# Two score products on the two halves of TensorE's rows, with 49 contracted rows each in place of 65

## The reference, cut to what matters

```python
# layer 0 (dist is (1, 512, 512), one scale per head)
scores = jnp.einsum('bhqd,bhkd->bhqk', q, k) / np.sqrt(hd)
scores = scores - torus_dist[:, None, :, :] * torus_scale[None, :, None, None]
scores = jnp.where(pad, NEG_INF, scores)
attn = jax.nn.softmax(scores, axis=-1)
# layer 1 (its mask lets in only keys of the last 128, for these inputs)
scores = jnp.einsum('bhnd,bhmd->bhnm', q, k) * scale
scores = jnp.where(mask, scores, -jnp.inf)
attn = jax.nn.softmax(scores, axis=-1)
```

## Time and profile before

| | before |
|---|---|
| median of 3 runs | 1530.71 us |
| the profiled execution | 1530.74 us |
| span of its trace | 1528.9 us |
| PE busy | 1372.1 us (90%) |
| DVE, ACT, POOL busy | 866.8, 803.0, 692.0 us |
| granted TensorE clock, mean | 0.96 |
| score matmuls L657 (layer 0) | 512, busy 205.3 us |
| score matmuls L703 (layer 1) | 512, busy 100.1 us |

### The profile page before, as it was taken

One profiled execution on the slowest core, in us unless ns is written; L12 is line 12 of the kernel. 1 busy time (PEld: TensorE's weight loads), 2 busy tenths in 40 slices (PEclk: granted clock), 3 DMA queues, 4 the chain that ended last, 5 costly groups with the idle time before them and its releaser, 6 DMA issues.

```text
span 1528.9 us, 25914 instructions
## 1 busy us (share of the span) xinstructions
PE 1372.1 (90%) x9365; PEld 1090.1 (71%) x9365; DVE 866.8 (57%) x2296; ACT 803.0 (53%) x1266; POOL 692.0 (45%) x856
## 2 busy tenths in 40 slices
PE   5898999999999999999999978898979888888867
PEld 3666777777777777777777767676767677767655
DVE  3766647548548457466556454647384746465551
ACT  3556655756746746656657526362535444453611
POOL 2788767758658758668768510101010101010110
PEclk9999999999999999999999989998999998999988
DMA  8654426325425534345263275856665747474510
GB/s 252 109 112 76 92 29 98 84 30 98 98 41 79 103 55 72 84 76 98 37 117 85 29 161 84 180 89 137 93 154 73 160 62 166 56 158 79 69 42 14
DMA packets 102537, 142.56 MB, mean 93 GB/s; under 512 B 22114, under 2 KB 49906, under 8 KB 102402
## 3 DMA queue, kind: packets, MB, share of 16 engines
q1 hardware_dynamic: 102402, 140.82, 49.6%
HBM read 98.27 MB, written 41.98 MB: 92 GB/s over the span
## 4 chain that ended last, share of the span: by engine, by line
PE 56%; DVE 18%; ACT 12%; POOL 7%; issue 3%; DMA 2%; SPq 1%; DVEq 0%; ACTq 0%; POOLq 0%
PE dense L589 15%; PE dense L569 13%; PE turned L669 9%; DVE shifted L1082 5%; PE pv L684 5%; PE score L657 4%; POOL shifted L472 3%; PE score L703 3%; ACT hidden L853 2%; PE turned L712 2%; POOL bias L465 2%; ACT L853 2%; DVE stats L968 2%; ACT L888 2%; DVE x_norm L978 2%
## 5 line engine op out<-in xcount | busy, mean ns | idle before, releaser
L1082 DVE CUSTOM_DVE_ANT_0 shifted<-score,bias 128x512 f32<-128x512 f32 x512 | 332.7, 687 | 258.4 <-PE score L657 156.8
L472 POOL TENSOR_SCALAR shifted<-shifted,row_max 128x512 f32<-128x512 f32 x512 | 358.3, 712 | 222.1 <-DVE row_max L1082 219.9
L872 ACT ACTIVATE probs<-turned 128x512 f32<-128x512 f32 x512 | 278.1, 596 | 213.3 <-PE turned L669 211.7
L669 PE MATMUL turned<-ident,shifted 128*128 128x128 f32 x2048 | 269.7, 274 | 7.5 <-POOL shifted L472 6.8
L669 PEld LDWEIGHTS turned<-ident,shifted 128*128 128x128 f32 x2048 | 233.3, 141 | 56.5 <-issue 26.7
L589 PE MATMUL dense<-w_down,hidden 128*128 128x256 f32 x1024 | 247.0, 385 | 12.1 <-ACT hidden L853 12.1
L465 POOL TENSOR_SCALAR bias<-dist,scale 128x1024 f32<-128x1024 f32 x192 | 218.4, 1138 | 21.0 <-DMA down_bias<-in_L_cond_b 21.0
L657 PE MATMUL score<-k_rows,q_rows 65*128 65x512 f32 x512 | 205.3, 456 | 23.6 <-DVE row_max L1082 10.5
L589 PEld LDWEIGHTS dense<-w_down,hidden 128*128 128x128 f32 x1024 | 185.6, 191 | 51.1 <-issue 16.3
L569 PE MATMUL dense<-feat_m,w_up 128*128 128x512 f32 x768 | 192.7, 404 | 8.4 <-DVE feat_m L1046 6.1
L888 ACT ACTIVATE probs<-turned 128x512 f32<-128x512 f32 x128 | 76.4, 597 | 202.8 <-PE turned L712 202.4
(11 more groups left out here) (114 smaller groups left out, 1556.6 us busy)
## 6 DMA issues: line engine op xcount, KB each, us to landing
q_rows<-qk_halves SPq DMA_DIRECT2D x256, 128.0 KB
k_rows<-qk_halves SPq DMA_DIRECT2D x256, 128.0 KB
qk_halves<-qk_high SPq DMA_DIRECT2D x64, 256.0 KB, 3.0
qk_halves<-qk_low SPq DMA_DIRECT2D x64, 256.0 KB, 3.0
x_in_t<-in_x SPq DMA_DIRECT2D x8, 512.0 KB, 3.6
x_res<-in_x SPq DMA_DIRECT2D x8, 512.0 KB, 8.3
x_mid<-x_norm SPq DMA_DIRECT2D x8, 512.0 KB, 3.5
x_in_t<-x_mid SPq DMA_DIRECT2D x8, 512.0 KB, 9.1
```

The costliest lines, as they stand in the source:

```text
L472: ins = pool.tensor_scalar(shifted[:, u % 3, i, :], shifted[:, u % 3, i, :], -1.0, row_max[:, t % 6:t % 6 + 1], ALU.mult, ALU.add)
L669: mm = pe.transpose(turned_bank[z % 2][:, HALF * kk + P * i:HALF * kk + P * i + P], shifted[:, u % 3, i, P * kt:P * kt + P], ident[:, :])
L872: act.activation(probs[:, u % RING, 2 * pair:2 * pair + 2, :], turned_bank[z % 2][:, :].rearrange("p (a c) -> p a c", a=2), ACT.Exp)\
L1082: dve.tensor_tensor_reduce(shifted[:, u % 3, i, :], score_bank[t % 2], bias[:, u % 2, i, :], 1.0, 3.0e38, ALU.add, ALU.min, row_max[:, t % ...
```

## The change

The product low·low is dropped: `TERMS` lists three combinations, so a score contracts 3 × 16 + 1 = 49 rows. These fit into one half of the partitions, and the operands now lie there twice: keys and mask on partitions 0 to 48 and again on 64 to 112 (a strip is 64 partitions); of the queries, even tiles lie on the first strip and odd tiles on the second. A unit's two matmuls take one strip each and write one bank each; so do the heads' four matmuls, in the order first, second, first, second. TensorE waits once per unit, until VectorE has read both tiles of the unit before. A group is now loaded with 12 DMAs for q (128 columns each), 6 for k and 2 for the mask. The ones of the mask row are set by two memsets of 32 partitions in place of one of a single partition, and the mask is built on partition 0.

```diff
-    KROWS = 4 * HD
+    TERMS = ((0, 0), (0, 1), (1, 0))
+    KROWS = len(TERMS) * HD
+    STRIP = P // 2
-    ROWS_LOADED = 9 * 16
+    ROWS_LOADED = 2 * (3 * len(TERMS) + 1) * 16
...
-        q_rows = sb("q_rows", [KROWS + 1, 2, HG, L], F32R)
-        k_rows = sb("k_rows", [KROWS + 1, 2, HG, L], F32R)
+        q_rows = sb("q_rows", [P, 2, HG, HALF], F32R)
+        k_rows = sb("k_rows", [P, 2, HG, L], F32R)
...
-                for r in range(4):
-                    sp.dma_start(q_rows[HD * r:HD * r + HD, g % 2, :, :].bitcast(F32),
-                                 qk_halves[m, r // 2, 0, rows, :].rearrange("(h e) n -> e h n", e=HD))\
+                for e in range(2):
+                    for r, (x, y) in enumerate(TERMS):
+                        at = slice(STRIP * e + HD * r, STRIP * e + HD * r + HD)
+                        for a in range(2):
+                            sp.dma_start(q_rows[at, g % 2, :, P * a:P * a + P].bitcast(F32),
+                                         qk_halves[m, x, 0, rows, P * (2 * a + e):P * (2 * a + e) + P]
+                                         .rearrange("(h e) n -> e h n", e=HD)).then_inc(loaded, 16)
+                        sp.dma_start(k_rows[at, g % 2, :, :].bitcast(F32),
+                                     qk_halves[m, y, 1, rows, :].rearrange("(h e) n -> e h n", e=HD))\
+                            .then_inc(loaded, 16)
+                    at = STRIP * e + KROWS
+                    sp.dma_start(k_rows[at:at + 1, g % 2, :, :].bitcast(F32),
+                                 mask_neg[:, :].bitcast(F32).unsqueeze(1).broadcast_to([1, HG, L]))\
                         .then_inc(loaded, 16)
...
             def scores(n, u):
                 g, half, j = u // 8, u // 4 % 2, u % 4
+                if n > 0 or u > 0:
+                    pe.wait_ge(s["scores_used"], TILES * n + 2 * u)
                 for i in range(2):
-                    t = 2 * u + i
-                    if n > 0 or t > 1:
-                        pe.wait_ge(s["scores_used"], TILES * n + t - 1)
-                    q0 = HALF * half + P * i
-                    pe.matmul(score_bank[t % 2], q_rows[:, g % 2, j, q0:q0 + P],
-                              k_rows[:, g % 2, j, :], start=True, stop=True).then_inc(s["scores_ready"], 1)
+                    at = slice(STRIP * i, STRIP * i + KROWS + 1)
+                    pe.matmul(score_bank[i], q_rows[at, g % 2, j, P * half:P * half + P],
+                              k_rows[at, g % 2, j, :], start=True, stop=True).then_inc(s["scores_ready"], 1)
...
                 for t in range(TT):
-                    mm = pe.matmul(score[:, t // 2, HALF * (t % 2):HALF * (t % 2) + HALF],
-                                   q_rows[:, g % 2, j, P * t:P * t + P], k_rows[:, g % 2, j, L - HALF:L],
-                                   start=True, stop=True)
+                    at = slice(STRIP * (t % 2), STRIP * (t % 2) + KROWS + 1)
+                    mm = pe.matmul(score[:, t % 2, HALF * (t // 2):HALF * (t // 2) + HALF],
+                                   q_rows[at, g % 2, j, P * (t // 2):P * (t // 2) + P],
+                                   k_rows[at, g % 2, j, L - HALF:L], start=True, stop=True)
```

More of the change, by code:

```diff
@@ L127, in build @@
         score_bank = [score[:, i, :] for i in range(2)]
-        head_scores = score[:, :, :].rearrange("p a b -> p (a b)").rearrange("p (t k) -> p t k", t=TT)[:, :, HALF - P:HALF]
+        head_scores = score[:, :, :].rearrange("p b (a k) -> p a b k", a=2)[:, :, :, HALF - P:HALF]
         turned_bank = [ps(f"turned{i}") for i in range(2)]
@@ L179, in build @@
         rstd = sb("rstd", [P, 2, TT])
-        mask_row = sb("mask_row", [KROWS + 1, L], U8)
-        mask_neg = sb("mask_neg", [KROWS + 1, L], F32R)
+        mask_row = sb("mask_row", [1, L], U8)
+        mask_neg = sb("mask_neg", [1, L], F32R)
         mask_col = sb("mask_col", [P, TT], U8)
@@ L294, in load_mask @@
                 rows = d["mask_BxS_bf1"] if m < B else d["mask_BxS_bk0"]
-                sp.dma_start(mask_row[KROWS:KROWS + 1, :], rows[m % B:m % B + 1, :]).then_inc(s["mask_loaded"], 16)
+                sp.dma_start(mask_row[:, :], rows[m % B:m % B + 1, :]).then_inc(s["mask_loaded"], 16)
                 if m >= B:
@@ L317, in load_group @@
                 rows = slice(HG * HD * g, HG * HD * (g + 1))
-                for r in range(4):
-                    sp.dma_start(q_rows[HD * r:HD * r + HD, g % 2, :, :].bitcast(F32),
-                                 qk_halves[m, r // 2, 0, rows, :].rearrange("(h e) n -> e h n", e=HD))\
-                        .then_inc(loaded, 16)
[L322 to L327, removed]
+                for e in range(2):
[11 more added lines that the diff above has]
+                                 mask_neg[:, :].bitcast(F32).unsqueeze(1).broadcast_to([1, HG, L]))\
+                        .then_inc(loaded, 16)
             def next_mask(m):
@@ L375, in prologue @@
                 load_x(1)
-                sp.wait_ge(s["ones_set"], 1)
+                sp.wait_ge(s["ones_set"], 2)
                 store_half(0, 0)
@@ L478, in mask @@
                 pad = -PAD if m < B else PAD
-                pool.tensor_scalar(mask_neg[KROWS:KROWS + 1, :], mask_row[KROWS:KROWS + 1, :], pad, -pad,
+                pool.tensor_scalar(mask_neg[:, :], mask_row[:, :], pad, -pad,
                                    ALU.mult, ALU.add).then_inc(s["mask_ready"], 1)
@@ L512, in prologue @@
                 pool.wait_ge(s["pool_consts"], 3)
-                pool.memset(q_rows[KROWS:KROWS + 1, :, :, :].bitcast(F32), 1.0).then_inc(s["ones_set"], 1)
-                pool.wait_ge(s["ones_set"], 1)
+                for e in range(2):
+                    pool.memset(q_rows[STRIP * e + 32:STRIP * e + STRIP, :, :, :].bitcast(F32), 1.0)\
+                        .then_inc(s["ones_set"], 1)
+                pool.wait_ge(s["ones_set"], 2)
                 mask(0)
@@ L761, in prologue @@
                 pe.wait_ge(s["value_ones"], 1)
-                pe.wait_ge(s["ones_set"], 1)
+                pe.wait_ge(s["ones_set"], 2)
             def turn(n):
@@ L1114, in shift_head @@
                 dve.wait_ge(s["scores_ready"], TILES * n + TT * h + TT)
-                dve.tensor_reduce(peak, head_scores, mybir.AxisListType.X, ALU.max).then_inc(s["peak_ready"], 1)
+                dve.tensor_reduce(peak.rearrange("p (a b) -> p a b", a=2), head_scores, mybir.AxisListType.X, ALU.max).then_inc(s["peak_ready"], 1)
                 dve.wait_ge(s["peak_ready"], H * (n - B) + h + 1)
-                dve.tensor_tensor(shifted[:, h % 3, 0, :].rearrange("p (t k) -> p t k", t=TT), head_scores,
-                                  peak.unsqueeze(2).broadcast_to([P, TT, P]), ALU.subtract)\
+                dve.tensor_tensor(shifted[:, h % 3, 0, :].rearrange("p (a b k) -> p a b k", a=2, b=2), head_scores,
+                                  peak.rearrange("p (a b) -> p a b", a=2).unsqueeze(3).broadcast_to([P, 2, 2, P]),
+                                  ALU.subtract)\
                     .then_inc(s["scores_used"], TT)
```

## The result

The changed kernel takes **1568.14 us** (median of 4 runs, 1565.12 to 1576.57) against 1530.49 for the kernel before (4 runs, 1529.92 to 1530.89): the ratio of their runs is 1.0255, 95% interval 1.0214 to 1.0296. It is slower by about 2.5%. The forecast was 1548 and slower; the loss came out as 37.6 us, more than twice the 17.3 of the sum. The profiled execution is the fastest of the four, 1565.12 us with a span of 1563.3.

A forecast was written before the change was run, and what follows sets the result against it. TensorE, busy 90% of the span, was taken to bound the kernel, though not everywhere. Layer 0 +15.1, layer 1 −0.8 and loads +3 summed to +17.3 us on 1530.74, so 1548 us; range 1482 to 1572.

The forecast's parts named there:

- the pair: Layer 0 score products on the chain: going into row strips costs 0.20 us, overlap of two products gains 0.225.
- the way out: Switch from row strips back to whole-array transposes behind a pair: 0.14 us; already paid where pv follows.
- the overlap: Two strips run at the same time, second product nearly free: gain 0.225 us per pair, bounds 0 and 0.235.
- the moved wait: Layer 0, pair starts after VectorE's second tile: VectorE's next tile about 0.61 us later where units run back to back.
- The start: First group's load on the chain, 20 DMAs in place of 9: +3 us, bounds 0 and 5.4.
- Later loads hidden: Groups after the first cost nothing: 9.6 us in hand against at most 5.4 more of issue time.
- Layer 1: Heads' products, eight after a wait and four without per pass: −0.8 us in all, bounds −14 and +7.
- The first two rivals: Row-strip switches cost nothing, 1489 us, chance 0.22; switches are paid and strips don't overlap, 1600 us, chance 0.12.
- the third: Rival: 49 rows run like 65, in one array, one after the other; 1541 us, chance 0.07.
- I count one place in a pass, +0.61: Layer 0: other work hides the moved wait in most units; one place per pass pays, bounds 0 and 1.5 us.
- the price of the strips in layer 0: Twelve pairs at +0.115 us and four with pv behind at −0.025: +1.28 us per pass.
- the clock in layer 0: Granted clock full in layer 0; a fall below 0.9 was named only as what would make the forecast wrong.

The follow-up runs named there:

- b_loads_only: Changed kernel's layout and 20 DMAs per group, products over all 128 partitions, wait per product, no strips, against the kernel before: 1529.97 us, ratio 1.0008.
- c_wait_only: Kernel before with only the wait moved: both products of a unit wait until VectorE has read both earlier tiles; 1553.07 us, ratio 1.0163.
- a_two_waits: Changed kernel with the old wait per product given back in layer 0, strips and loads kept: 1551.25 us, ratio to the kernel before 1.0155.
- d_one_strip: Changed kernel with all products of a unit or head on the first strip, so switches paid without overlap: 1631.66 us, ratio to the kernel before 1.0675.
- e_wait_light: Kernel before with the moved wait in only nine units of each layer 0 pass, those after steps with little TensorE work: 1550.38 us, ratio 1.0149.
- g_gap: Kernel before without the low-low term, its rows zero, still 65 rows on the whole array, 7 DMAs per group: 1522.12 us, ratio 0.9961.

## Why the prediction was wrong

**Right.** Slower, and for the reasons named, but with less than half of the size. The prices per instruction hold: the pair 0.20 − 0.225 (0.43 against 0.47 in the chain), the way out 0.14 (1.02 against 0.88), nothing more where pv follows, the overlap 0.23 (0.66 against 0.43), the moved wait 0.61 at a place. The start: +3 forecast, +2.0 measured. Later loads hidden: b_loads_only gives 1.0008 in all. Layer 1: −0.8 forecast, −3.0 in one trace, within what wobbles there. The first two rivals fall, by the 1.02 and by the 0.43; the third falls too, since 49 rows did not run like 65.

The Trainium skill's "TensorEngine Tiling (Array Packing)", section Tiling Modes, has it that a change of tiling mode drains the engine. The trace agrees that the change has a price, now for rows too: 0.14 us more behind the pair, and about 0.19 on the way in (0.43 − 0.235 − 0.005, or 0.66 − 0.47 with one strip). How much of each is a drain and how much weights that are loaded late, no run separates. The Trainium skill's "TensorE: Matmul & The Clock Gate", Part 3, gives a packed group the time of one matmul plus about 4 ns for each further tile. The trace agrees: the busy time of two products together is 0.50 us, that of one 0.498. Only it is not the price of the group in a program that changes mode around it.

**Wrong: the count of places for the moved wait.** The step was "I count one place in a pass, +0.61", with a high bound of 1.5. Alone the wait costs 3.3 us in an ordinary pass and 27.9 in layer 0 (c_wait_only), where 4.9 in all were forecast. The argument was that most units have more than 1.4 us of other work in between on TensorE or VectorE. But TensorE stands ahead of twelve of the 32 pairs. Ahead of units 1, 2, 4, 6, 17, 19, 21, 23 and 25 it has too little other work, and ahead of units 5, 20 and 24 VectorE is late, so work on TensorE does not help. The chain of waits hid this from me: it shows other engines there, GpSimd and ScalarE, and I took a wait of TensorE's that is off the chain for one that can grow at no cost. The rows were there to count: per unit, the distance between its first product and the next one's, when VectorE starts, and what it needs for two tiles.

**Wrong, by less: the price of the strips in layer 0.** The forecast had 1.28 us per pass, 10.2 in all. The strips alone cost 1.9 in an ordinary pass and 18.7 in all, of which some 3.5 are the clock of two passes. In the second pass of a_two_waits, units 8 to 14 and 26 to 30 lengthened by 0.09 to 0.13 each, as forecast (units 11 and 27, with pv, by −0.03). The excess is in units 16 to 25, 0.8 us together, 0.34 of it in unit 25, whose pair the chain of before did hold. Why a pair there costs more than the sum of its switches was not tried. The number of pairs was not at fault: the chain of before holds 14 whole pairs and four single products in the third pass, and 17 units lengthen in d_one_strip.

**Left out: the clock in layer 0.** The prediction kept it at full and named a fall only as a sign of being wrong. In the changed kernel three later passes hold a stretch at half clock and are 1.5 us longer for it, and the first has a granted clock of 0.92 where before it had 0.96. Three times 1.5 is 4.4 of the 35.4 us.

The two parts don't add: in the second pass 1.9 + 3.3 = 5.2, and the changed kernel loses 3.95, since a unit that waits for VectorE doesn't notice the switch (16, 18, 20, 22, 24 take 2.0 us with or without strips). The forecast for a pass was 1.89.

The range, 1482 to 1572, held the median, and this was luck: it reached so far only to cover the other cases and high bounds for the switch, while the wait's own bound was less than half of what was measured, and one of the four runs, 1576.57, lies outside.

## What to carry to other kernels

When a wait is moved from one buffer to a pair of buffers, lay out a whole period step by step and count the steps in which the engine on the other side ends later than the work in between, because that work is short or because that engine itself starts late. There the two engines take turns, at up to 0.6 us each time here. Better, keep one wait per buffer: the strips worked with it and lost 17 us less, though they still lost 20. When parts are tried apart, compare single passes with the same granted clock before adding up whole runs; here e_wait_light looked like all of the wait's price and was two thirds of it. Strips of the array pay only if what is saved on the products exceeds one way in and one way out for each visit, 0.19 + 0.14 = 0.33 us here against 0.23 saved: a pair of short products between full-array work is too little. And a term can be left out without changing the shape of the product; the lighter loads were worth 0.4% here.

## What the runs showed of the hardware

Two things that I had not expected.

The granted clock falls in layer 0 too. Two passes of the changed kernel, the third and the fourth, each from its first product to the next pass's (columns as above):

```profile
248.20:359.70 111.50, 103.29 (x801) 75.42 (x800) 62.99 (x195) 65.89 (x110) 77.91 (x97) 1.00 0.27 77
359.70:472.70 113.00, 104.84 (x801) 76.53 (x800) 62.80 (x195) 66.00 (x110) 78.00 (x97) 0.98 0.28 76
```

They do the same work, and the second has a stretch at half clock (1.2 instead of 2.4 GHz) behind two idle times of TensorE close together, 1.10 us ahead of the transposes of an x_norm and 0.56 us ahead of the pair of unit 6, and is 1.5 us longer. Both passes have 107.6 us and clock 1.00 in the kernel before. That longer waits make such a stretch more likely is not borne out by the other runs: c_wait_only, with the wait in every unit, has a stretch in one later pass, e_wait_light, with the wait in nine, in six, and g_gap, with no wait moved, in one. That their number differs from run to run would explain why the changed kernel spreads over 11 us (mean clock 0.960 in the fastest run, 0.956 in the slowest), but it was not tried apart.

The DMA engines are busy for less time with the 20 DMAs of a group than with the 9, though these carry more. The page of the changed kernel has

```profile
DMA packets 154255, 151.57 MB, mean 97 GB/s; under 512 B 32610, under 2 KB 109554, under 8 KB 154114
q1 hardware_dynamic: 154114, 149.77, 35.8%
```

against 142.56 MB in 102537 packets and a share of 49.6% before: more bytes, half as many packets again, and less time. The loads differ in that q comes in pieces of 512 bytes in place of 2 KB, and in the partitions that they write. The small pieces alone are not the answer: in the fourth pass a packet of 2 KB took 114 ns on average, where one of the same size took 196 before. What made them shorter is open. SyncE's wait for a group to land before the next mask fell too,

```profile
SPq L340 <- DMA k_rows<-mask_neg: 19.0, 8, 2.7
```

from 48.2 us in 8 times. It bought nothing here, since the later loads are hidden. It may be why 11 more DMAs cost the start only 2 us and not the 5.4 that SyncE needs to issue them; this was not tried.
